# A graph network of two layers: three buffers, not two, for the one-hot bytes that layer 1's edge stage writes

## The reference

```python
def _egnn_conv(x, src, dst, edge_attr, W_msg, W_edge, W_root, b):
    msg = x[src] @ W_msg + edge_attr @ W_edge
    agg = jax.ops.segment_max(msg, dst, num_segments=x.shape[0])
    agg = jnp.where(jnp.isneginf(agg), 0.0, agg)
    return agg + x @ W_root + b
c1 = jax.nn.leaky_relu(_egnn_conv(X, src, dst, edge_attr, W1_msg, W1_edge, W1_root, b1))
c2 = jax.nn.leaky_relu(_egnn_conv(c1, src, dst, edge_attr, W2_msg, W2_edge, W2_root, b2))
out = _layernorm(x + c2, axis=-1)
```

## Time and profile before

| | |
|---|---|
| runs | 1887.03, 1889.02 and 1883.07 us; median 1887.03 |
| profiled execution, span | 1876.7 us |
| PE busy | 1519.6 us, 81% |
| DVE busy | 1313.2 us, 70% |
| POOL busy | 1084.8 us, 58% |
| ACT busy | 1080.4 us, 58% |
| HBM traffic | 283.25 MB read, 173.37 MB written |

### The profile page before, as it was taken

One profiled execution on the slowest core, in us unless ns is written; L12 is line 12 of the kernel. 1 busy time (PEld: TensorE's weight loads), 2 busy tenths in 40 slices (PEclk: granted clock), 3 DMA queues, 4 the chain that ended last, 5 costly groups with the idle time before them and its releaser, 6 DMA issues.

```text
span 1876.7 us, 37108 instructions
## 1 busy us (share of the span) xinstructions
PE 1519.6 (81%) x11422; PEld 1348.9 (72%) x11422; DVE 1313.2 (70%) x2383; ACT 1080.4 (58%) x2450; POOL 1084.8 (58%) x1454
## 2 busy tenths in 40 slices
PE   3998888988889888886889888988987767676763
PEld 3677777777778888885778777777777667666662
DVE  3677676777665555553667767677736899999998
ACT  2354444545443455553555555555535888888887
POOL 6777777767600000002777777777757787675663
PEclk9999999999999999998999999999998998988887
DMA  7779999999865777885788888888867899999996
GB/s 145 203 213 266 271 266 263 264 276 273 245 226 169 226 248 261 279 277 189 204 225 228 238 229 235 226 223 242 223 223 215 267 290 298 296 299 296 294 300 176
DMA packets 505022, 459.13 MB, mean 245 GB/s; under 512 B 348553, under 2 KB 412340, under 8 KB 504836
## 3 DMA queue, kind: packets, MB, share of 16 engines
q1 hardware_dynamic: 444118, 321.15, 59.9%
q0 software_dynamic: 30976, 57.72, 12.7%
q10 hardware_dynamic: 29742, 77.88, 10.6%
HBM read 283.25 MB, written 173.37 MB: 243 GB/s over the span
## 4 chain that ended last, share of the span: by engine, by line
PE 30%; DVE 25%; DMA 19%; POOL 15%; issue 9%; ACT 1%; SPq 1%; POOLq 0%; DVEq 0%; ACTq 0%
PE ps L570 18%; DMA onehot_bytes<-arena 14%; POOL arena L397 13%; DVE stats L937 6%; DVE arena L880 4%; DMA arena<-nodes,src_perm 4%; DVE arena L935 4%; DVE arena L932 4%; PE ps L482 4%; POOL onehot L430 2%; PE ps L450 2%; PE ps L473 2%; PE ps L443 2%; DVE arena L955 2%; DVE arena L866 1%
## 5 line engine op out<-in xcount | busy, mean ns | idle before, releaser
L570 PE MATMUL ps<-hold,onehot 128*128 x4688 | 612.7, 293 | 186.2 <-POOL onehot L430 139.5
L570 PEld LDWEIGHTS ps<-hold,onehot 128*128 128x128 f32 x4688 | 582.3, 205 | 217.0 <-issue 216.8
L397 POOL DMA_INDIRECT arena<-nodes,src_perm x392 | 370.0, 944 | 473.4 <-SPq L364 354.2
L482 PEld LDWEIGHTS ps<-w_root,onehot 97*128 97x128 f32 x3136 | 400.9, 194 | 99.7 <-issue 97.5
L397 POOL DMA_INDIRECT arena<-in_x_dram,src_all x392 | 374.4, 955 | 143.0 <-issue 114.3
L482 PE MATMUL ps<-w_root,onehot 97*128 97x128 f32 x3136 | 417.6, 277 | 0.0
L430 POOL CAST onehot<-keep 128x256 f32<-128x256 uint8 x588 | 298.8, 556 | 115.5 <-PE ps L570 72.4
L634 ACT COPY arena<-ps 128x384 f32<-128x384 f32 x392 | 187.5, 478 | 274.2 <-PE ps L482 272.4
L684 ACT COPY arena<-ps 128x384 f32<-128x384 f32 x392 | 166.6, 477 | 208.6 <-PE ps L570 208.5
L866 DVE TENSOR_TENSOR_SCAN arena<-keep,arena,ps 96x512 f32<-96x512 bf16 x196 | 247.7, 1264 | 46.6 <-PE ps L450 46.2
L880 DVE TENSOR_TENSOR onehot<-count,rel 128x1024 f32<-128x1024 bf16 x147 | 179.5, 1222 | 142.3 <-PE ps L570 141.2
(11 more groups left out here) (97 smaller groups left out, 1158.4 us busy)
## 6 DMA issues: line engine op xcount, KB each, us to landing
root<-arena ACTq DMA_DIRECT2D x196, 384.0 KB
arena<-root SPq DMA_DIRECT2D x196, 384.0 KB, 4.4
nodes<-arena SPq DMA_DIRECT2D x98, 384.0 KB, 2.7
arena<-nodes SPq DMA_DIRECT2D x98, 384.0 KB
arena<-in_x_dram SPq DMA_DIRECT2D x97, 384.0 KB
arena<-in_x_dram SPq DMA_DIRECT2D x48, 768.0 KB, 8.0
out_dram<-arena SPq DMA_DIRECT2D x48, 768.0 KB, 4.6
onehot_bytes<-arena SPq DMA_DIRECT2D x147, 128.0 KB
```

What stands on the lines that cost most here:

```text
L397: nc.gpsimd.indirect_dma_start(out=gathered[t.ring][0:t.p, i, 0:D], out_offset=None, in_=table_in, in_offset=bass.IndirectOffsetOnAxis(ap= ...
L482: last = nc.tensor.matmul(no_ps[m % 2][:, i * P:(i + 1) * P], nodes_t[m % NODE_RING][0:D + 1, i * P:(i + 1) * P], w_root[0:D + 1, layer * ...
L570: nc.tensor.matmul(ps_bytes[:, bass.ds(place_at, SLOT)].bitcast(F32), onehot[:, k % NS, i, :], flat[:, bass.ds(chunk_at, P)], start=False, ...
```

## The change

`bytes_out` has three buffers in the place of two. The first two lie where they lay, in `arena`; the third is a new array `tail` of 1024 bytes a partition. `stats` and `small`, which only the second merge uses, have no arrays of their own now and lie in `tail`. A batch k is written to buffer k % 3 and waits for the store of batch k - 3; there are three semaphores for the stores, and SP waits for all three before layer 2.

```diff
-        stats = sb("stats", [P, RI, 6], F32)
-        small = sb("small", [P, 9, RI], F32)
+        tail = sb("tail", [P, 2 * P], F32)
...
-        bytes_out = arena[:, at_rest + 4 * GE:at_rest + 4 * GE + 2 * BW // 4].bitcast(U8).rearrange("p (i n) -> p i n", n=BW)
+        assert BW // 4 == 2 * P and RI * 6 + 9 * RI <= 2 * P
+        bytes_out = [arena[:, at_rest + 4 * GE + i * BW // 4:at_rest + 4 * GE + (i + 1) * BW // 4].bitcast(U8) for i in range(2)] + [tail[:].bitcast(U8)]
+        stats = tail[:, 0:RI * 6].rearrange("p (j c) -> p j c", c=6)
+        small = tail[:, RI * 6:RI * 15].rearrange("p (c j) -> p c j", j=RI)
...
-        bytes_stored, bytes_in = sems("bytes_stored"), sems("bytes_in")
+        bytes_stored, bytes_in = sems("bytes_stored", 3), sems("bytes_in")
...
-                sp.dma_start(onehot_dram[k // 2][:, k % 2 * BW:(k % 2 + 1) * BW], bytes_out[:, k % 2, :]).then_inc(bytes_stored[k % 2], DMA)
+                sp.dma_start(onehot_dram[k // 2][:, k % 2 * BW:(k % 2 + 1) * BW], bytes_out[k % 3]).then_inc(bytes_stored[k % 3], DMA)
...
-            for i in range(2):
-                sp.wait_ge(bytes_stored[i], DMA * ((NBATCH + 1 - i) // 2))
+            for i in range(3):
+                sp.wait_ge(bytes_stored[i], DMA * ((NBATCH + 2 - i) // 3))
...
-                if k >= 2:
-                    dve.wait_ge(bytes_stored[k % 2], DMA * (k // 2))
-                compare(bytes_out[:, k % 2, :].rearrange("p (t n) -> p t n", n=P), k, count_ps).then_inc(bytes_made, 1)
+                if k >= 3:
+                    dve.wait_ge(bytes_stored[k % 3], DMA * (k // 3))
+                compare(bytes_out[k % 3].rearrange("p (t n) -> p t n", n=P), k, count_ps).then_inc(bytes_made, 1)
```

More of the change, by code:

```diff
@@ L945, in finish @@
                 nc.vector.tensor_tensor(diff, even, odd, ALU.subtract)
-                next_step(nc.vector.tensor_reduce(both, stats[:].rearrange("p j (h c) -> p j c h", c=3)[:, :, 1:3, :], mybir.AxisListType.X, ALU.add))
+                next_step(nc.vector.tensor_reduce(both, stats.rearrange("p j (h c) -> p j c h", c=3)[:, :, 1:3, :], mybir.AxisListType.X, ALU.add))
                 then(nc.vector.scalar_tensor_tensor(diff, diff, 0.25, diff, ALU.mult, ALU.mult))
```

## The result

The changed kernel takes 1859.18 us (median of 5 runs, 1853.53 to 1860.44) against 1887.03 us (median of 5 runs, 1879.45 to 1889.02): a ratio of 0.985, interval 0.983 to 0.987, so 27.9 us faster. The forecast was 1865, 22 us faster. The time lies in the stated range (1858 to 1877), 1.2 us from its fast end, and outside the 1860 to 1871 of the forecast's own case; a gain above 27 us was the case that I had given 4 in 100.

The account below looks back on a forecast made before the run. The loop of compares and byte stores was taken to bound layer 1's edge stage, POOL next. Gains of 17.3 (pace), 4 (lag) and 1 (tail) sum to 22.3, taken as 22: 1865 us, range 1858 to 1877.

Parts of the forecast that it names:

- the forecast's own case: Layer 1's edge stage: POOL's gathers become the bound; gain 16 to 27 us, so 1860 to 1871 us; chance 0.66.
- the case that I had given 4 in 100: Gain above 27 us: PE recovers all 8.4 us of lag and the tail gives 1.7; chance 0.04.
- Part 1: Layer 1's edge stage: with the third buffer, DVE's 109.4 us of store waits and PE's 51.2 us go.
- Part 2: Layer 1's edge stage: gathers at layer 2's step, so the last starts at 501.8, not 519.1: 17.3 us sooner.
- Part 3: End of layer 1's edge stage: PE recovers its lag behind POOL; 4 us taken, bounds 0 and 8.4.
- Part 4: After layer 1's last turn: DVE's and PE's short waits before the merge go; 1 us gained, bounds 0 and 1.7.
- Parts 5 and 6: SP's store order and semaphore waits: nothing lost; placing `stats` and `small` in `tail`: price 0, bounds -1 and +1 us.
- From span to median: Whole kernel: the median was 10.3 us above the profiled span; the same distance turned 1854.7 into 1865.
- B: Layer 1's edge stage: DMA is the second bound, limiting the gain to 9 to 14 us, 1873 to 1878; chance 0.18.
- C: Byte loop: the wait only moves, stores slow from 4.73 to 7.7 us, time stays 1887 within 0.3%; chance 0.07.
- D: Byte loop: stores beyond 7.7 us make three buffers slower; at 8.2 us, 1911; chance 0.05 with the port lock.
- the shared port between VectorE and GpSimd: Edge stage: DVE's compares might lock GpSimd out and delay gathers, some 74 us, so 1939; chance 1 in 100.

## Why the prediction was right, and where its sizes were off

The mechanism held: the wait two stores back was the bound, and POOL's pace is the next. The size did not: 22 us were forecast and 27.9 came. That the time still lay in the range, by 1.2 us, is in part luck, since single runs of the changed kernel went from 1853.53 to 1860.44.

*The bound before* was the loop of two compares and a store: shown by the old wait with three buffers (no gain) and by three gathers with two buffers (5.16 us a group in place of 5.215). My count of the stores on the chain was slightly off: 59.7% of 433.1 us are 259 us, which are 55 stores of 4.70 us, not 57 of 4.73. Nothing hangs on the difference.

*Part 1, the waits go:* 109.4 us were forecast to fall under 10, and 31.4 stayed. I had left a store's duration as it was, and stores got slower. Over those of 110 to 500 us whose landing the trace holds in full, the mean is 4.2 us before and 5.4 after. Whether the busier engines (270 and 286 GB/s) or the third store in flight did it, no run separates. The mean stayed under the 7.2 us at which the loop would have been POOL's equal, and what the compare still waited reached PE with 3.6 us. The conclusion held, the size of this sign did not.

*Part 2, POOL's pace:* 17.3 us forecast, 501.8 for the last gather; measured 502.2 and 501.2. The step was 1.249 us as in layer 2. That POOL is the bound is shown by taking the bytes away (nothing gained) and by taking gathers away (4.63 us a group in place of 5.00).

*Part 3, the lag, is the term that was mis-sized.* I took 4 us between 0 and 8.4, with the argument that the DMA engines had no room for the catching up. The last turn follows the last gather by 7.1 and 4.8 us now; in the three profiles with the old wait it was 13.5, 16.0 and 16.8. That is 9.5 us on average. The bound of 8.4 came from a single execution whose lag was the smallest of the three. And the room that I had denied was there: in 110 to 160 us, with the bytes begun at 111, the engines moved 293 GB/s at a share of 0.97, and the first wait of PE for a gather falls between 150 and 170 us, so PE had caught up 40 to 60 us after the bytes began. The run with doubled stores shows a condition under which my 0 would have been about right. Recovering the lag in full was what the case with a chance of 4 in 100 stood for, and it is what happened.

*Part 4, the tail:* 1 us forecast; 15.4 us now, 15.6 to 16.7 before. *Parts 5 and 6:* nothing forecast, nothing found. By the sign that I had named, a longer second merge (499.9 and 497.1 us against 494.6), part 6 would have been wrong, but the sign was a poor one: with `tail` in the same place the second merge took 493.8 and 492.3 us in the runs that wait two stores back, so that the sign showed scatter.

Sum by the averages of the profiles: 17.5 for the last gather, 9.5 for the lag and 0.6 for the tail, 27.7 us before rounding, where I had 17.3 + 4 + 1 = 22.3.

*From span to median* was a mistake in its own right. I took the 10.3 us between the profiled span (1876.7) and the median (1887.03) as time that lies outside the span. In the five runs of the changed kernel the time is 1.8 us above the span each time (1859.9 and 1858.1 in the profiled one). So the profiled execution of before was itself some 8 us below the median, and what I carried over was scatter. It did no harm, since I subtracted the gain from both ends alike.

*Rivals.* B (DMA as the second bound) wanted a step of 1.26 to 1.29 us at a share of 0.95 or more; the share was 0.95 and the step 1.249. Only the run with 227 KB more a group lost time, and not in the pace. C and D needed stores of 7.7 us on average; the average is 5.4, and the longest on the chain is 6.42 in the first profile of the changed kernel and 7.44 in the second. Of the shared port between VectorE and GpSimd (the Trainium skill, "SBUF — State Buffer", section "SBUF: two separate sides"): the second profile of the changed kernel has 315 gathers of 929 to 955 ns beside the same compares in less time, and leaving the compares out changed POOL's busy time by 0.1 us in 100. So this compare held up no gather. The one gather of 1100 ns in the first profile's row starts at 108.67, before the first compare at 111.43, beside DVE's small table operations, as did the one of 1.44 us before.

## What to carry to other kernels

A buffer more is worth the distance to the next bound, not the waits it removes: here taking away 78 of 109 us of waits was worth 28 us, and the second bound's pace could be read from another stage of the same kernel that already ran at it. Add to the pace what had piled up behind the old bound (here PE's lag of three groups), and take that lag from more than one profile. Once one engine sets the pace, the others' slack can be spent: work moved from the tail into the loop gave another 14 us, though it is worth less while the old bound stands.

## What the runs showed of the hardware

The DMA engines' busy share was a poor measure of what they could still take. At 0.93 and 270 GB/s one would think of a ceiling near 290; the same mix with further 128 KB stores ran at 321 GB/s with a share of 1.00. The duration of a store grew beside the load: 4.2 us on average at 270 GB/s and 5.4 at 286 with a third in flight. POOL's indirect gathers kept a median of 944 to 947 ns and a gap of 0.30 us in every run, with DMA between 238 and 321 GB/s.
